# Which engine issues the loads of the q/k/v weights for the first three sub-tiles: ScalarE instead of GpSimd

## What is computed

```python
qkv = x @ w_qkv;  q, k, v = jnp.split(qkv, 3, axis=-1)
q = elu(q) + 1;   k = elu(k) + 1;   kv = k * v
# per decay d in (sigmoid(alpha), sigmoid(beta)), over time t:
#   run[t] = d * run[t-1] + z[t]      for z = kv and z = k
den = clip(sum(q * run_k, axis=-1), 1e-6)
out = concat([q * run_kv_f / den_f, q * run_kv_s / den_s]) @ w_out
x = layernorm(x + out)
h = silu(x @ wg.T) * (x @ wu.T)       # int32 weights, scale 1/127
x = layernorm(x + h @ wd.T)
```

## Time and profile before

| | us |
|---|---|
| three runs | 2690.82 (median), 2687.62, 2901.44 |
| profiled execution, its own time | 2690.82 |
| its span (core 0, the slowest) | 2689.3 |
| spans of the other cores | 2659.4 to 2688.1 |
| granted TensorE clock, mean by core | 0.913 to 0.920 |
| PE busy / DVE / ACT / POOL | 1735.2 / 854.7 / 598.4 / 488.5 |

### The profile page before, as it was taken

How to read it: one execution, slowest core, us unless ns; L and a number is a source line. 1 busy time by engine, 2 the same in 40 slices (tenths; PEclk the granted TensorE clock), 3 DMA queues, 4 the chain that set the end, 5 groups by cost and what they waited for, 6 DMA issues and landing times.

```text
span 2689.3 us, 21182 instructions; the slowest of 8 cores (2659.4 to 2689.3 us)
## 1 busy us (share of the span) xinstructions
PE 1735.2 (65%) x7153; PEld 732.5 (27%) x7298; DVE 854.7 (32%) x1010; ACT 598.4 (22%) x632; POOL 488.5 (18%) x500
## 2 busy tenths in 40 slices
PE   0000014378777887778778878787778877778586
PEld 0000001133333333333333333333333333333232
DVE  0000014434433443254324431453234414451111
ACT  0000002113312332233223321322133212331111
POOL 5500003312210222022202220222021202211000
PEclk9999997689988998899889988899989989899898
DMA  8999961073247323733364326532563256314433
GB/s 102 112 114 109 109 105 47 28 180 117 67 117 199 113 88 96 189 133 98 86 168 150 114 73 156 164 124 59 157 172 102 62 161 178 102 59 142 128 106 114
DMA packets 247180, 316.07 MB, mean 118 GB/s; under 512 B 91171, under 2 KB 173092, under 8 KB 244772
## 3 DMA queue, kind: packets, MB, share of 16 engines
q1 hardware_dynamic: 215332, 201.44, 27.2%
q0 software_dynamic: 22528, 96.49, 19.9%
q10 hardware_dynamic: 9216, 16.78, 1.7%
HBM read 318.80 MB, written 54.53 MB: 139 GB/s over the span
## 4 chain that ended last, share of the span: by engine, by line
PE 50%; another core or an unknown queue 14%; DVE 14%; ACT 11%; issue 5%; DMA 3%; POOL 1%; SPq 1%; DVEq 0%; ACTq 0%; POOLq 0%
PE C_ps L720 10%; PE D_ps L720 10%; PE A_ps L447 7%; DVE runs L523 6%; PE A_ps L775 3%; PE B_ps L775 3%; PE C_ps L775 3%; PE D_ps L775 3%; ACT sgb L730 3%; ACT L730 2%; PE C_ps L591 2%; PE A_ps L591 2%; PE B_ps L591 2%; PE D_ps L591 2%
## 5 line engine op out<-in xcount | busy, mean ns | idle before, releaser
L447 PE MATMUL A_ps<-xT,wq_buf 128*128 128x512 bf16 x1002 | 265.3, 421 | 459.5 <-DMA wq_buf<-wq_s 362.2
L720 PE MATMUL C_ps<-y1T,wg_buf 128*128 128x512 bf16 x1505 | 393.6, 417 | 128.6 <-ACT sgb L730 91.7
L720 PE MATMUL D_ps<-y1T,wu_buf 128*128 128x512 bf16 x1504 | 344.6, 379 | 4.6 <-DVE hbuf L737 1.6
L447 PEld LDWEIGHTS A_ps<-xT,wq_buf 128*128 128x128 bf16 x1024 | 106.2, 106 | 615.9 <-issue 526.2
L545 POOL TENSOR_TENSOR runs<-qb,runs 128x1024 f32<-128x1024 f32 x64 | 148.7, 2343 | 670.5 <-DVE states_sb L532 670.5
L720 PEld LDWEIGHTS C_ps<-y1T,wg_buf 128*128 128x128 bf16 x1536 | 159.6, 106 | 361.6 <-issue 225.7
L737 DVE TENSOR_TENSOR hbuf<-D_ps,sgb 128x1024 bf16<-128x1024 f32 x96 | 117.6, 1225 | 367.6 <-ACT sgb L730 367.3
L298 POOL DMA_DIRECT2D wq_buf<-wq_s x192 | 104.6, 569 | 573.4 <-PE A_ps L447 507.9
L720 PEld LDWEIGHTS D_ps<-y1T,wu_buf 128*128 128x128 bf16 x1536 | 149.2, 98 | 187.3 <-issue 9.3
L358 POOL TENSOR_TENSOR denr<-qb,runs 128x1024 bf16<-128x1024 f32 x64 | 150.1, 2346 | 222.3 <-PE B_ps L370 222.1
L470 DVE SCALAR_TENSOR_TENSOR kphi<-ebuf,kphi 128x1024 f32<-128x1024 f32 x32 | 39.2, 1225 | 461.5 <-ACT kphi L467 461.5
(11 more groups left out here) (80 smaller groups left out, 1710.2 us busy)
## 6 DMA issues: line engine op xcount, KB each, us to landing
wq_buf<-wq_s POOLq DMA_DIRECT2D x192, 256.0 KB, 3.3
wg_buf<-wg_s SPq DMA_DIRECT2D x192, 256.0 KB, 3.0
wu_buf<-wu_s SPq DMA_DIRECT2D x192, 256.0 KB, 4.1
wd_buf<-wd_s SPq DMA_DIRECT2D x384, 128.0 KB, 2.3
wo_buf<-wo_s SPq DMA_DIRECT2D x256, 128.0 KB, 2.9
out<-work ACTq DMA_DIRECT2D x64, 256.0 KB, 5.3
xbf<-x POOLq DMA_DIRECT2D x32, 256.0 KB, 177.7
xbm<-xbf POOLq DMA_DIRECT2D x32, 256.0 KB, 4.5
```

Of the source, the lines that this page charges most:

```text
L447: t.matmul(o, a, b, start=f1, stop=f2),
L720: t.matmul(o, a, b, start=f1, stop=f2),
```

## The change

The six first loads and the refills of wq_buf are issued by ACT for sub-tiles 0, 1 and 2, and by POOL from sub-tile 3 on. The loads by POOL get semaphores of their own (`ch_wq_g`). What is loaded, when in program order, and what a load waits for stay as they are.

```diff
+    ch_wq_g = [mkch(f"ch_wq_g{i}") for i in range(3)]
...
     def stream_chunk2(sg, key, buf, scratch, src4, slot_g, cval, ci,
                       q="sync"):
         sl = ci % 3
-        wch = ch_w[key][sl]
+        wch = ch_wq_g[sl] if (key == "wq" and q == "gpsimd") else ch_w[key][sl]
...
     def emit_A(sg):
         s, st = divmod(sg, NST)
+        wq_q = "gpsimd" if sg >= 3 else "scalar"
         for ci in range(3):
             stream_chunk2(sg, "wq", wq_buf, wq_s, wq_in, wq_slot_g,
-                          wq_cval, ci, q="gpsimd")
+                          wq_cval, ci, q=wq_q)
...
             if mi % 2 == 1 and ci + 3 < 12:
                 stream_chunk2(sg, "wq", wq_buf, wq_s, wq_in, wq_slot_g,
-                              wq_cval, ci + 3, q="gpsimd")
+                              wq_cval, ci + 3, q=wq_q)
```

## The result

The changed kernel takes 2587.67 us against 2703.68 us (medians of twelve executions each, side by side), a ratio of **0.957 (95% interval 0.954 to 0.960)**, 116 us less. Forecast were 123 us less. (In some executions of either kernel one die shows a lower granted clock and takes longer; ratio and interval are from those without this.) The profiled execution took 2591.05 us, span 2589.5 on core 5; beside the span of 2689.3 that is only 100 us less, because it took longer than most executions of its kernel, and the one of before less than most of its own.

A forecast was written before the change was run, and what follows sets the result against it. A(0)'s wq loads, queued behind conversions it doesn't need, were taken to bound the start. The gain of 145 us to B(0)'s end less 22 us lost on ACT made 123: 2690.8 to 2568 us, range 2540 to 2640.

The forecast's parts named there:

- The waiting load as the bound: Start of A(0): wq loads wait in q0 behind conversions; first matmul at 372.82 us, near 70 us once ACT issues them.
- The pace: A(0)'s loads beside conversions: queues alternate by packets, 1.30 us a turn, 11.7 us a load; B(0) starts at 367 us.
- the second of these steps: B(0): conversions end at 392 us, then 24 missing wo halves take 25 us; B(0) ends at 417 us.
- One sign: Start, sub-tile 0: ACT's wq loads land 60 us and more after issue.
- The gain: Up to B(0)'s end: 417 us instead of 561.5, 145 us won.
- Turns by bytes: Rival, A(0)'s loads: queues share by bytes, 24 us a load; net gain 46 us, 2645 us; chance 0.10.
- one packet a load: Rival, A(0)'s loads: each takes 2.5 us, B(0) starts at 212 us; net gain 260 us, 2431 us; chance 0.03.
- no overtaking: Rival, start: DMA engines are full until 371 us, A(0) starts as before, ACT's 22 us are lost; 2713 us; chance 0.05.
- Slower: Rival, whole run: ACT's place in line costs 40 us, A(0) gains little, from about 55 us a load; 2711 us; chance 0.02.
- The loss on ACT: Sub-tiles 0 and 1, before A(1) and A(2) and in C: loads in ACT's order cost 11 us each, 22 us for two.
- 5.7 were priced: Between B and C, after normalization: two ACT issues of 0.58 us and some 4.5 us to landing before A(1)'s first matmul.
- 2.3 us were priced: C stage: in two pairs a sub-tile, refill issues before the exp of k delay q matmuls 1.16 us each.

The follow-up runs named there:

- rows_4k: Changed kernel, ACT issuing only sub-tile 0's wq loads, two wq tiles per DMA with 4 KB rows; no ratio on record, B(0) from 235.2 to 411.4 us.
- rows_1k: Changed kernel, ACT issuing only sub-tile 0's wq loads, each split into two with 1 KB rows instead of 2 KB; ratio 0.974 to the kernel before.
- refill_act: Changed kernel, but in sub-tiles 1 to 7 POOL issues the first six wq loads and ACT the refills; ratio 0.954 to the kernel before.

## Why the prediction was right

**The waiting load as the bound: right.** A(0) waited for its place in q0, not for data: put elsewhere, the first matmul ran at 71.9 us ("near 70").

**The pace: right, and quick enough.** 1.30 us a turn, 11.7 us a load were read from 510 packets of another tile's loads, and measured as just that. B(0) was to start at 367 (368.6 on the mean core), the conversions to end at 392 (389.6), B(0) at 417 (414.2). One sign missed: the loads were to land 60 us and more after issue, and the median is 55.5.

What fixes the gain is the second of these steps, the end of the conversions and the wo halves still missing then. The pace had only to bring B(0) to its start before that: with a start at 235 us instead of 362 B(0) ended no sooner (rows_4k), with one at 458 it ended at 487.9 (rows_1k). The forecast took 216 packets at 0.1 us, 21.6 us of delay for the conversions; they ended 20.9 us later than before (389.6 against 368.7, mean core).

The gain was to be 145 us and is 144.6. That this agrees to half a microsecond is luck: B(0) ended 2.8 us before its forecast, but in the kernel before it also ended 2.7 us before the 561.5 us of core 0 from which the forecast was counted (558.8 on the mean core).

**The rivals.** Turns by bytes is refuted by the row lengths; the same counts, 1232 to 1234 and 1298 to 1298, refute one packet a load; no overtaking falls with the first matmul. "Slower" needed a pace of 55 us a load.

**The loss on ACT: right in place, too small in size.** The term was 22 us for two sub-tiles; it is 32, so the stages give 112 us net where 123 were forecast. C(0) and C(1) were to start 34.9 and 34.6 us after the end of B; it was 35.4 and 35.5. (The steps written down for C(0) add up to about 596 us rather than 596.4; that changes nothing.) Core 5, sub-tile 1: the end of the normalization, ACT's issues right behind it, and A(2)'s first matmul:

```profile
726.62 0.29 ACT L661 ACTIVATE stat<-stat,cv_sb 128x2 f32<-128x2 f32 x1
726.63 15.51 ACTq L299 DMA_DIRECT2D wq_buf<-wq_s  x8
...
734.89 5.88 PE L449 MATMUL A_ps<-xT,wq_buf 128*128 128x512 bf16 x16 [22.61 <-DMA wq_buf<-wq_s]
```

From issue to matmul it is 8.3 us here, 6.3 to 9.1 over all cores and both sub-tiles, and 7.6 and 7.2 on the mean core, where 5.7 were priced; of that 0.5 and 0.9 us show in the stretch from B to C. As much again comes from the yardstick: core 0, on which the price was worked out, took 26.4 and 25.9 us for the stretch in the kernel before, the mean core 25.6 and 24.9. In C 2.3 us were priced and 3.8 to 4.8 came: the issue's delay was right in kind (0.84 us of wait, where two issues were priced at 1.16 us), but a wait that pushes PE down to the low clock has a second price, 1.7 us a group, and the working had none for it. In refill_act these slow groups account for the missing part. (The last 3 us of the 32 lie in B(1) and B(2), 2.3 us, and were not looked into.)

**What the prediction did not say** is that the change is quicker without its second half. Sub-tiles 1 and 2 gain nothing from ACT: with the loads back on POOL, A(1)'s first matmul comes 3.3 to 4.8 us after B(0)'s end instead of 21 to 23, and the stretch to B(3) is back at 793.7 us.

## What to carry to other kernels

When a load waits, look at which queue it stands in and what stands before it, and only then at bandwidth: the same engines gave these loads a place every 1.3 us as soon as they had a queue of their own. While a queue with big packets is full, price a load by its number of packets, longer rows being cheaper for the same bytes, and follow the next stage too, since it may wait for the same queues and give back all that was won. Move only the loads that stand behind the jam, since in the program of a computing engine each issue has a place, and a delay of under a microsecond behind it (0.84 us here) can cost PE its clock as well.

## What the runs showed of the hardware that was not expected

A wait raised from 1.5 to 2.3 us let the matmul group behind it run at the low of TensorE's two clock levels (1.2 instead of 2.4 GHz; mostly 5.3 us instead of 3.6 for 16, with part of the group at either) in 66 of 92 cases. In the start, where PE works in groups mostly 9 to 21 us apart, the page's slices show a granted clock of 0.5 to 0.7. The last q group of A(0) took 6.26 us there instead of 3.61, which is 2.7 us on B(0)'s start; on its end, which follows the conversions, no cost shows.

In the hardware queues a row counts as a packet at 1, 2 and 4 KB alike, and each DMA has one small packet an engine more: 18, 9 and 4.5 packets an engine for a tile of 256 KB. A conversion DMA in q0 has one packet of 16 KB written, which is eight rows, and a small one, as long as the rows it writes follow one another in DRAM; in rows_4k, where they don't, it wrote packets of 2 KB. The Trainium skill (DMA: Bandwidth & Descriptors, Queues, rings and completion order) gives about 9 to 17 descriptors as typical for a packet, all sent before an engine turns to another queue; by that the eight rows of a load could go in one turn, and the traces show one row a turn (1232 packets of q0 beside 1234 of q10).
